# A convolution, attention and mixture-of-experts chain on one core: the order of small matmuls, and who adds the pairs of one attention unit, changed at five places

## What is computed

```python
# L0: 1x1 convolutions; softmax over the last axis v of the energies
q, k = wq@x + bq, wk@x + bk          # 16 channels each, per image
v = wv@x + bv                        # 128 channels
energy = einsum('bci,bcj->bij', q, k).reshape(b, h, w, h, w)
x = gamma * einsum('bchk,bhwkv->bcwv', v, softmax(energy, -1)) + x
# L1: tokens t; _ln = (t - mean) / sqrt(var + eps) over the 128 channels
k, q, v = (_ln(t) @ W).reshape(B, N, 8, 16)     # for Wk, Wq, Wv: 8 heads of 16
scores = einsum('bnhd,bmhd->bnmh', k, q) / sqrt(16)
t = t + einsum('bnmh,bmhd->bnhd', softmax(scores, over m), v)
# L1 FFN: 8 experts of width 512, the two best by logits = _ln(t) @ gate_w.T
h = gelu(_ln(t) @ w1[e].T + b1[e]);  y = h @ w2[e].T + b2[e]
t = t + sum over e of comb[:, e] * y
```

## Time and profile before

| | us |
|---|---|
| median of 3 runs | 186.28 |
| the three runs | 186.28, 186.07, 189.12 |
| the profiled execution, its own time | 186.13 |
| its span, first to last instruction | 184.2 |
| TensorE busy | 174.1 (95% of the span) |
| ScalarE busy | 123.2 (67%) |
| VectorE busy | 117.1 (64%) |
| GpSimd busy | 79.5 (43%) |

### The profile page before, as it was taken

One profiled execution on the slowest core, in us unless ns is written; L12 is line 12 of the kernel. 1 busy time (PEld: TensorE's weight loads), 2 busy tenths in 40 slices (PEclk: granted clock), 3 DMA queues, 4 the chain that ended last, 5 costly groups with the idle time before them and its releaser, 6 DMA issues.

```text
span 184.2 us, 3336 instructions
## 1 busy us (share of the span) xinstructions
PE 174.1 (95%) x1277; PEld 118.6 (64%) x1277; DVE 117.1 (64%) x199; ACT 123.2 (67%) x185; POOL 79.5 (43%) x68
## 2 busy tenths in 40 slices
PE   6999999989898998999999999999999999999991
PEld 3267867665466544447466567567887888888880
DVE  1569544985465396456084959397888677676673
ACT  3516953317727743545988598867878999999970
POOL 8404228988703284452536093524151152333312
PEclk9999999999999999999999999999999999999999
DMA  5799200000000000570000000000000880000001
GB/s 141 276 374 419 96 0 0 4 0 4 0 5 0 2 0 4 181 271 7 0 0 5 0 0 0 4 0 0 0 7 4 244 269 0 0 4 0 0 0 57
DMA packets 5791, 10.94 MB, mean 59 GB/s; under 512 B 1280, under 2 KB 1664, under 8 KB 5520
## 3 DMA queue, kind: packets, MB, share of 16 engines
q1 hardware_dynamic: 5360, 10.65, 16.7%
q10 hardware_dynamic: 416, 0.08, 0.3%
HBM read 10.17 MB, written 0.56 MB: 58 GB/s over the span
## 4 chain that ended last, share of the span: by engine, by line
PE 73%; issue 8%; ACT 7%; POOL 4%; DVE 4%; DMA 2%; ACTq 0%; DVEq 0%; POOLq 0%
PE PS L1159 9%; PE PS L1163 7%; PE PS L1160 7%; PE PS L1186 6%; PE PS L1189 6%; PE PS L1187 6%; PE PS L1181 4%; POOL pairs L357 4%; PE PS L1017 3%; PE PS L1031 3%; ACT room L516 2%; PE PS L910 2%; PE PS L878 2%; PE PS L1104 2%; DMA convw_sb<-convw 2%
## 5 line engine op out<-in xcount | busy, mean ns | idle before, releaser
L516 ACT ACTIVATE room<-PS,b_sb 128x512 f32<-128x512 f32 x64 | 43.6, 688 | 22.6 <-PE PS L1163 21.2
L772 DVE TENSOR_TENSOR Gl<-room,Gh 128x512 fp32r<-128x512 f32 x50 | 41.2, 831 | 13.7 <-ACT Gh L461 13.0
L365 POOL TENSOR_TENSOR x_sb<-x_sb,room 128x512 f32<-128x512 f32 x15 | 23.6, 1572 | 56.0 <-DVE room L781 56.0
L1159 PE MATMUL PS<-x2h,w1h 128*128 128x512 f32 x64 | 27.4, 427 | 1.2 <-ACT room L516 0.8
L461 ACT ACTIVATE Gh<-room 128x512 fp32r<-128x512 f32 x40 | 25.3, 633 | 1.3
L1163 PE MATMUL PS<-x2l,w1h 128*128 128x512 f32 x64 | 25.5, 398 | 0.0
L1160 PE MATMUL PS<-x2h,w1l 128*128 128x512 f32 x64 | 25.2, 393 | 0.0
L1186 PE MATMUL PS<-Gh,w2h 128*128 128x512 f32 x50 | 20.8, 416 | 0.0
L1187 PE MATMUL PS<-Gh,w2l 128*128 128x512 f32 x50 | 19.8, 395 | 0.0
L1189 PE MATMUL PS<-Gl,w2h 128*128 128x512 f32 x50 | 19.7, 395 | 0.0
L1159 PEld LDWEIGHTS PS<-x2h,w1h 128*128 128x128 f32 x64 | 12.0, 187 | 10.6 <-issue 4.9
(11 more groups left out here) (136 smaller groups left out, 294.2 us busy)
## 6 DMA issues: line engine op xcount, KB each, us to landing
room<-comb_rows SPq DMA_DIRECT2D x16, 256.0 KB, 5.2
w1raw<-w SPq DMA_DIRECT2D x8, 256.0 KB, 5.9
w_sb<-w SPq DMA_DIRECT2D x2, 1024.0 KB, 10.6
x_sb<-x SPq DMA_DIRECT2D x2, 256.0 KB, 3.2
dev<-xk SPq DMA_DIRECT2D x1, 512.0 KB, 6.3
out<-x_sb SPq DMA_DIRECT2D x2, 256.0 KB, 4.2
attw_sb<-attw SPq DMA_DIRECT2D x1, 320.0 KB, 6.8
cst<-consts SPq DMA_DIRECT2D x1, 228.5 KB, 6.5
```

Source lines behind the costliest of these rows:

```text
L365: nc.gpsimd.tensor_tensor(t2[:, cols(p)], t2[:, cols(p)], part[:, s, :], ALU.add).then_inc(acc_done, 1)
L516: nc.scalar.activation(G[:, n % GR, :], PS[:, U_BANK[n % 2], :], ACT.Gelu, bias=b1_sb[:, c:c + 1])\
L772: nc.vector.tensor_tensor(Gl[:, n % GR, :], G[:, n % GR, :], Gh[:, n % GR, :].bitcast(f32), ALU.subtract)\
L1159: mm(o, w1h[e][:, ms], x2h[:, cols(p)], start=True, stop=False)
```

## The change

1. Convolution: q's projection reads x in its natural order; the copies L425 and L588 read PSUM through `by_columns` (a step of 16 elements) instead. Five turns and one bias matmul stand ahead of the energies, the second bias and both halves of v among them, three turns behind.
2. First attention: `project_second(2)` stands ahead of `raw_scores(1)`. The maxima of image 0 are transposed into bank 1 instead of bank 0, so they wait for copies of k and q and no longer for v's copy; the first `scores` waits for that.
3. Unit 2's halves are added by VectorE (a new `pair` in its list, behind `image_max_rows(1)` and ahead of `attend(0)`), into `early_pairs`, a part of `room` that the convolution has left; GpSimd adds those of units 0, 1, 4 to 7. Unit 3 stays unpaired. `scores(3, 0)` moves ahead of `sums(0)` and `sums(1)`, and its waits and those of unit 2 go by step.
4. FFN: unit 4's scores stand behind `up(11)`; `project_v(1)` goes from step 10 into bank 6 at step 12, behind that step's `down`s, and waits for unit 4's exponentials; ScalarE's copy of it goes to step 12 too.
5. `low_weights2` starts two steps later and its first waits for `comb_ready` 1.

```diff
+        early_pairs = room[:, 0:4 * TOK].rearrange("p (j t) -> p j t", j=4)
...
+        def by_columns(images):
+
+            return images.rearrange("c (b h w) -> c b w h", b=2, h=H)
...
-        PAIRED = [True, True, True, False, True, True, True, True]
-        NMT_BANK = [((0, 0), (0, TOK)), ((2, 0), (3, 0))]
+        POOL_PAIRS = [0, 1, 4, 5, 6, 7]
+        NMT_BANK = [((1, 0), (1, TOK)), ((2, 0), (3, 0))]
...
-        V_BANK = [0, 2]
+        V_BANK = [0, 6]
...
-        LATE_SCORES = (19,)
+        LATE_SCORES = (11, 19)
         HEADS_AT = {0: (2, 3)}
-        VALUES_AT = 10
+        VALUES_AT = 12
...
-        LOW_W2 = {n + 1: e for n, e in enumerate(W2_ORDER)}
+        LOW_W2 = {n + 3: e for n, e in enumerate(W2_ORDER)}
...
                     pool.wait_ge(sums_done, 4)
+                    pool.wait_ge(comb_ready, 1)
...
-            for u in range(3):
+            for u in range(2):
                 for s in range(2):
                     pair(u, s)
...
-                nc.scalar.activation(cq[0:C8, pair, :, :, 0].rearrange("c b w h -> c (b w h)"), PS[64:64 + C8, p, :],
+                nc.scalar.activation(cq[0:C8, pair, :, :, 0], by_columns(PS[64:64 + C8, p, :]),
...
-                nc.vector.tensor_scalar(cq[32:32 + C8, pair, :, :, 1].rearrange("c b w h -> c (b w h)"),
-                                        PS[64:64 + C8, p, :], convb_sb[64:64 + C8, 0:1], None, ALU.add)\
+                nc.vector.tensor_scalar(cq[32:32 + C8, pair, :, :, 1], by_columns(PS[64:64 + C8, p, :]), convb_sb[64:64 + C8, 0:1], None, ALU.add)\
...
+            def pair(u, s):
+
+                j = slice(2 * s, 2 * s + 2)
+                dve.wait_ge(prob_ready, 2 * u + s + 1)
+                nc.vector.tensor_tensor(pairs_of(u)[:, j, :], probs_of(u)[:, j, 0, :], probs_of(u)[:, j, 1, :],
+                                        ALU.add).then_inc(dve_paired, 1)
...
             image_max_rows(1)
+            for s in range(2):
+                pair(2, s)
             attend(0)
...
-                mm(PS[64:64 + C8, p, :].rearrange("c (b w h) -> c b w h", b=2, w=W),
-                   convw_sb[:, 0:C8], x_sb[:, cols(p)].rearrange("c (b h w) -> c b w h", b=2, h=H),
-                   start=True, stop=True)
+                mm(PS[64:64 + C8, p, :], convw_sb[:, 0:C8], x_sb[:, cols(p)], start=True, stop=True)
...
                 if p:
-                    pe.wait_ge(part_ready, 1)
+                    pe.wait_ge(prob_ready, 10)
...
-                    pe.wait_ge(v_ready, 2)
+                    pe.wait_ge(act_kq_ready, 6)
...
+                if u == 0 and s == 0:
+                    pe.wait_ge(v_ready, 2)
...
-                if u == 2 and s == 0:
+                if u == 2 and s == 1:
                     pe.wait_ge(prob_ready, 3)
-                if u == 3 and s == 0:
-                    pe.wait_ge(prob_ready, 5)
+                if u == 3:
+                    pe.wait_ge(prob_ready, 4 + s)
...
+                if u == 5:
+                    pe.wait_ge(v_ready, 2 * NHALF)
```

More of the change, by code:

```diff
@@ L173, in hybrid_program @@
         score_done, prob_ready, paired, pv_done = sem("score_done"), sem("prob_ready"), sem("paired"), sem("pv_done")
-        sums_done = sem("sums_done")
+        sums_done, dve_paired = sem("sums_done"), sem("dve_paired")
         rcp_ready, att_ready, t2_ready = sem("rcp_ready"), sem("att_ready"), sem("t2_ready")
@@ L262, in norm_tiles, with pairs_of @@
             return range(cols.start // 128, cols.stop // 128)
+        def pairs_of(u):
+            return early_pairs if u == 2 else pairs[:, u % 2]
         def paired_by(u, s):
-            return 2 * sum(PAIRED[:u]) + s + 1
+            return 2 * POOL_PAIRS.index(u) + s + 1
         def raw_slot(n):
@@ L354, in pair @@
                 pool.wait_ge(prob_ready, 2 * u + s + 1)
-                if u >= 2:
+                if u >= 4:
                     pool.wait_ge(sums_done, u - 1)
-                nc.gpsimd.tensor_tensor(pairs[:, u % 2, j, :], probs_of(u)[:, j, 0, :], probs_of(u)[:, j, 1, :],
+                nc.gpsimd.tensor_tensor(pairs_of(u)[:, j, :], probs_of(u)[:, j, 0, :], probs_of(u)[:, j, 1, :],
                                         ALU.add).then_inc(paired, 1)
@@ L888, in conv_values @@
                               start=False, stop=True, skip_group_check=True)
-                    if k % 4 == 1:
-                        turn(1)
                 last.then_inc(vT_done, 1)
@@ L1112, in sums @@
                 pe.wait_ge(prob_ready, 2 * u + 2)
-                if PAIRED[u]:
+                if u in POOL_PAIRS:
                     pe.wait_ge(paired, paired_by(u, 1))
+                else:
+                    pe.wait_ge(dve_paired, 2)
                 if g == 0 and b >= 2:
@@ L1117, in sums @@
                     pe.wait_ge(prob_ready, 4 * b + 4)
-                for mt in range(1 if PAIRED[u] else 2):
-                    for j in range(4):
-                        addend = pairs[:, u % 2, j, :] if PAIRED[u] else probs_of(u)[:, j, mt, :]
-                        last = mm(PS[head_rows(j), SUM_BANK[b], 0:TOK], ones_par[:, g, :], addend,
-                                  start=(g == 0 and mt == 0), stop=(g == 1), skip_group_check=True)
+                for j in range(4):
+                    last = mm(PS[head_rows(j), SUM_BANK[b], 0:TOK], ones_par[:, g, :], pairs_of(u)[:, j, :],
+                              start=(g == 0), stop=(g == 1), skip_group_check=True)
                 last.then_inc(sums_done, 1)
@@ L1175, in down @@
                         pe.wait_ge(combT_ready, 1)
-                    if k == 2:
-                        pe.wait_ge(v_ready, 2 * NHALF)
                 y, ms = PS[:, Y_BANK[k % 2], :], slice(m * 128, (m + 1) * 128)
@@ L1189, in down @@
                 mm(y, w2h[e][:, ms], Gl[:, n % GR, :], start=False, stop=(m == MT - 1)).then_inc(down_done, 1)
+            turn(5)
+            conv_bias(0)
+            energy(0)
             turn(1)
-            for i in range(2):
-                conv_bias(i)
-            for q in range(WQ):
-                energy(q)
-                turn(1)
-            for i in range(2):
-                conv_values(i)
-            turn(2)
+            energy(1)
+            conv_bias(1)
+            energy(2)
+            conv_values(0)
+            energy(3)
+            conv_values(1)
+            turn(3)
             conv_apply(0)
@@ L1221, in _ @@
             project_second(1)
+            project_second(2)
             raw_scores(1)
-            project_second(2)
             project_second(3)
@@ L1235, in _ @@
             scores(2, 1)
+            scores(3, 0)
             sums(0)
             sums(1)
-            scores(3, 0)
             scores(3, 1)
@@ L1269, in _ @@
                     project_other(h)
-                if n == VALUES_AT:
-                    project_v(1)
                 for p in range(NHALF):
@@ L1283, in _ @@
                     down(d)
+                if n == VALUES_AT:
+                    project_v(1)
                 if n in ATTENDS:
```

## The result

| | before | after |
|---|---|---|
| median of 6 runs, us | 186.27 | 183.33 |
| range, us | 185.95 to 189.12 | 182.67 to 183.82 |
| profiled execution, its own time | 186.13 | 183.82 |
| its span | 184.2 | 181.9 |
| TensorE busy | 174.1 | 173.6 |

The ratio is 0.9845 with a 95% interval of 0.9813 to 0.9877: 2.9 us faster (2.3 to 3.5). The two profiled executions differ by 2.31 us only, since the profiled one of the changed kernel is the slowest of its six. In some executions TensorE's granted clock falls for a while; the ratios leave out only those over 1.5% above the fastest (189.12 us, say) and keep milder ones (187.5), so some ratios have beside them the mean over the undisturbed executions alone (mean granted clock 0.994 or more). For the whole change these means are 186.14 and 183.26, 2.88 us apart.

A forecast was written before the change was run, and what follows sets the result against it. TensorE, busy 95% of the span, was taken as the bound, with gains only where it idles or works slowly; 0 - 0.8 - 0.65 - 0.55 = -2.0 us gave 184.1 profiled, 184.2 on the median, range 183.0 to 185.7.

The forecast's parts named there:

- first rival: Convolution: q projection gets shorter in natural order, 183.3 if TensorE is faster from 6 us, 182.5 if throughout; chance 0.15.
- Convolution, 0: Convolution: reading x in natural order frees nothing, energies start at 9.75 us as before; gain 0.
- The length goes by the columns and not by the step: Convolution, q's projection: a pass's time depends on its column count, so the step of 16 elements costs nothing measurable.
- second rival: Convolution, q's copies: reading PSUM with a step costs time, 185.6 at twice the length, 187.7 at three times; chance 0.12.
- First attention, -0.8: First attention: earlier projection, VectorE's pairs and early scores bring the norm, and so the FFN's start, 0.8 us forward.
- Part (a): First attention: project_second(2) falls into a wait, so VectorE's maximum of image 1 comes at 37.3, not 37.77: -0.5 us.
- step (c): First attention: sums(2) starts at 49.25, TensorE reaches norm_center(4) at 54.05, 0.8 us earlier; its own work decides.
- (b): First attention, VectorE: unit 2's pairs end by 48.45, both attends follow, attend(1) done at 53.9 against 54.8 us.
- third rival: First attention: VectorE's pairs come late or slow, or TensorE's work moves nothing; 184.5 to 185.0 us, chance 0.15.
- Routing, -0.65: FFN routing: with GpSimd's splits waiting for comb, the third raw_heads starts at 69.2 instead of 69.87 us; gain 0.65.
- Steps 10 to 13, -0.55: FFN: up(11) runs where v's projection stood, up(13) starts at 91.8 instead of 92.36 us; gain 0.55.
- fourth rival: FFN: a wait only moves, ScalarE's gelu late again at step 13 or v's copy holding unit 5; 184.8 us, chance 0.08.

The follow-up runs named there:

- e1: Kernel before with all of the convolution's edits alone, q's copies included: median 185.64 us against 186.29, ratio 0.9957.
- e12: Kernel before with only the order of turns, biases and halves of v in the convolution changed, q's projection still stepped: ratio 0.9988.
- e6: Changed kernel with unit 2's pairs given back to GpSimd: ratio to the kernel before 0.9844.
- e11: Kernel before with q's projection and copies in natural order, turns and biases as they were: ratio 0.9986.
- e10: Changed kernel with three turns replaced by four unread q projections, two natural, two stepped, executed once: passes 0.43 us apart natural, 0.85 stepped.
- e4: Kernel before with up(11) ahead of unit 4's scores and v's projection at step 12, alone: ratio 0.9960.
- e8: Kernel before with GpSimd's w2 splits one step later and no wait for comb_ready: 186.63 us against 186.13, ratio 1.0030.

## Why the prediction was right, and where not

184.2 in a range of 183.0 to 185.7 was forecast, 183.33 measured. The range holds because it was drawn to take in half of the first rival; the main case, 183.7 to 184.7, does not. The sum of the stages was -2.0, the traces show -2.31, and the medians -2.9. The 0.6 between the last two is the convolution, put at 0; that the two profiled executions show it at 0 too is luck, as both have a late rise of the clock.

- *Convolution, 0*: right in the profiled execution (+0.05), wrong in the mean (0.6 us for e1; 0.3 to 1.3 by its ratio). The step that failed is "The length goes by the columns and not by the step". It was read at TensorE's lower level, where a stepped pass costs 0.83 to 0.86 us like an unbroken one. In the kernel before the clock may rise in mid-projection without the passes of q showing it, since at the upper level the step holds a pass at 0.85: q to E is 5.67 or 5.68 in six stepped executions with the old layout, and 5.74 in e12. In natural order it was 4.48, 4.70, 4.78, 4.93, 5.15, 5.68 and 5.74, by the moment of the rise. The comparison with the k projections had a second flaw: by the code these read runs of 128 elements, not every second one, so they were no case of a step at all. The first rival (0.15) had this mechanism, and its 183.3 for a rise at 6 us is the measured time by luck, as the attention and steps 10 to 13 gave 0.35 more than their terms. What the Trainium skill says of a penalty for each new line (SBUF — State Buffer, Door 1: The DMA port swizzle) holds at the upper level, 0.85 against 0.43, and shows nothing at the lower.
- *Copies with a step in PSUM, no cost*: right, 0.71 and 0.75 us as before. The second rival is out.
- *First attention, -0.8*: 1.02. Part (a) was over by 0.12 (`raw_scores(2)` at 36.27, not 36.1), and step (c) wrong in two places: `sums(2)` started at 49.59 and not at 49.25, but from there to `norm_center(3)` TensorE took 52.75 - 49.59 = 3.16 us and not the 3.75 of the earlier trace rows, which held a wait for unit 3's exponentials that I had not separated. So not TensorE's work but `attend(1)` decides, at 53.9 as (b) had it; by e6 TensorE's sums stand only 0.08 us behind it. The third rival is out.
- *Routing, -0.65*: 0.64.
- *Steps 10 to 13, -0.55*: 0.68. v's projection costs 0.81 and not 0.9, and `up(11)` ended before the rows of maxima, as forecast. The fourth rival is out.
- *Nothing behind 90 us is fixed*: 91.8 us from `up(13)` to the end in all kernels.

## What to carry to other kernels

Take the clock's level into account before an access pattern is called free: a pass at the lower level hides what the upper one pays (0.85 us with the step at either, 0.43 without it at the upper), and the gain of a repaired pattern then comes in some executions and not in others, which one trace cannot show. Where several small operations of VectorE form a chain on a critical path, keep long GpSimd additions off the whole chain by a wait for its last result; shifting them by a step made it worse here. Between two stages, look for the work that can run in the wait of the next (here an `up`, a projection, an early score) rather than for a faster engine: handing the pairs to VectorE was worth 0.08 us, the order of the scores 0.66.

## What the runs showed of the hardware

- TensorE reaches its upper level (2.4 GHz) between 4.78 us (e1) and 7.58 us (e11), although in all 14 traces its first work starts at 1.48 us and is the same up to the projections. The granted clock reads 1.00 all the while, since the trace's list of clock states only begins with the rise; the lengths of the passes show it, 0.63 and then 0.38 us for one of k.
- An fp32 pass of 512 columns whose moving operand steps over 16 elements takes 0.85 us at the upper level (e10, e4, e12) against 0.43 unbroken, and 0.84 to 0.86 against 0.83 to 0.86 at the lower. Reading PSUM with the same step costs ScalarE and VectorE nothing (0.71 and 0.75 us for 16x512).
- The granted clock can fall in the convolution although TensorE is busy, here in the products of v and the turns among them, from 15.2 to 18.6 us, to the lower level. In the profiled execution of e4_vlater (busy us by engine, then clock, DMA share, GB/s):

```profile
8.00:16.00 8.00, 8.00 (x139) 5.14 (x138) 5.91 (x11) 2.77 (x5) 1.06 (x1) 0.95 1.07 392
16.00:24.00 8.00, 7.77 (x133) 6.84 (x136) 4.92 (x10) 5.70 (x11) 2.11 (x2) 0.84 0.45 185
```

  Its stage from the energies to `norm_center(4)` is 1.5 us longer for it (46.65 against 45.15). With the new order of turns and halves of v this was seen in 1 of 47 executions, with the old in 40 of 130.
- Beside w2's splits on GpSimd, small VectorE operations can last until the split beside them ends, each held by one split of its own: in e8 1.05 and 1.21 us for two operations of 0.16 and 0.19. The two ahead of them in the chain were not held (0.18 us each).
